# Building an adjacency matrix from one-hots: GpSimd takes over a third of the cell one-hots, and its additions move one group later

## The reference

```python
Z = jnp.matmul(X, W)
msg = Z[edge_src] * edge_vals[:, None]
agg = jax.ops.segment_sum(msg, edge_dst, num_segments=X.shape[0])
return jax.nn.relu(agg)
```

## Time and profile before

| | us |
|---|---|
| median of the runs shown (three) | 1432.24 |
| lowest and highest of them | 1429.69, 1436.95 |
| the profiled execution's own time | 1431.51 |
| its span, first to last instruction | 1429.8 |
| mean granted clock of TensorE | 0.979 |

### The profile page before, as it was taken

One profiled execution on the slowest core, in us unless ns is written; L12 is line 12 of the kernel. 1 busy time (PEld: TensorE's weight loads), 2 busy tenths in 40 slices (PEclk: granted clock), 3 DMA queues, 4 the chain that ended last, 5 costly groups with the idle time before them and its releaser, 6 DMA issues. The chain is left out here.

```text
span 1429.8 us, 23949 instructions
## 1 busy us (share of the span) xinstructions
PE 1365.1 (95%) x7919; PEld 892.0 (62%) x7920; DVE 771.4 (54%) x1622; ACT 457.2 (32%) x1133; POOL 261.9 (18%) x365
## 2 busy tenths in 40 slices
PE   9999999999999999999998999999989999889994
PEld 4688864455457777777555677767535555556661
DVE  7999965572158888877474333333360011643336
ACT  3599940021045555555112111111170012121110
POOL 1133320000000000000021555555200000005540
PEclk9999999999999999999999999999999999889996
DMA  6000000040000000000503999999510000543326
GB/s 159 30 0 0 0 0 0 0 180 0 0 30 2 2 1 2 1 2 1 162 15 95 328 317 316 320 322 306 173 54 0 0 0 0 174 164 96 102 82 227
DMA packets 84195, 131.01 MB, mean 92 GB/s; under 512 B 11865, under 2 KB 49135, under 8 KB 83733
## 3 DMA queue, kind: packets, MB, share of 16 engines
q1 hardware_dynamic: 70303, 108.72, 23.1%
q0 software_dynamic: 12032, 18.17, 4.0%
q10 hardware_dynamic: 1788, 3.16, 0.8%
HBM read 115.33 MB, written 29.56 MB: 101 GB/s over the span
## 5 line engine op out<-in xcount | busy, mean ns | idle before, releaser
L1267 PEld LDWEIGHTS ps<-b_r 128*128 128x128 f32 x1024 | 125.9, 194 | 34.5 <-issue 33.0
L1267 PE MATMUL ps<-b_r 128*128 128x78 f32 x1024 | 123.9, 275 | 2.0 <-DVE b_r L1344 1.3
L1276 PE MATMUL ps<-b_r 128*78 128x512 f32 x256 | 121.2, 596 | 0.0
L592 PE MATMUL ps<-b_r 125*125 125x160 f32 x660 | 118.4, 315 | 0.0
L1171 POOL TENSOR_TENSOR b_x<-b_x,b_r 125x512 f32<-125x512 f32 x10 | 12.7, 1267 | 534.5 <-DVE b_r L1121 534.5
L507 ACT ACTIVATE b_r<-b_r 125x125 f32<-125x125 f32 x330 | 107.6, 389 | 9.2 <-DVE b_r L402 4.8
L942 PEld LDWEIGHTS ps<-b_r 125*64 125x64 f32 x1600 | 85.3, 136 | 24.6 <-issue 22.8
L1327 ACT ACTIVATE b_r<-ps,b_r 128x78 f32<-128x78 f32 x128 | 34.7, 323 | 205.1 <-PE ps L1267 171.4
L905 PE MATMUL ps<-b_r 64*125 64x417 f32 (+1 forms) x480 | 95.4, 529 | 1.4 <-DVE ps L1034 1.2
L942 PE MATMUL ps<-b_r 125*64 125x125 f32 x1600 | 94.7, 272 | 1.3 <-ACT b_r L970 1.3
L592 PEld LDWEIGHTS ps<-b_r 125*125 125x125 f32 x660 | 92.0, 187 | 1.1
(11 more groups left out here) (272 smaller groups left out, 2224.3 us busy)
## 6 DMA issues: line engine op xcount, KB each, us to landing
b_r<-L_ffn_w SPq DMA_DIRECT2D x128, 512.0 KB
b_r<-y SPq DMA_DIRECT2D x20, 512.0 KB, 7.2
b_r<-L_ffn_W SPq DMA_DIRECT2D x2, 4096.0 KB, 20.4
y<-b_r SPq DMA_DIRECT2D x2, 2500.0 KB
rows<-b_r SPq DMA_DIRECT2D x2, 2400.0 KB
b_x<-x SPq DMA_DIRECT2D x5, 480.0 KB
out<-b_x ACTq DMA_DIRECT2D x5, 480.0 KB
b_w_a<-L_gnn_W SPq DMA_DIRECT2D x2, 512.0 KB, 9.3
```

Source lines behind the costliest of these rows:

```text
L592: last = pe.matmul(T.ps[:P, 2 + b, 0:WC], T.weighted[:, b, j, :], T.cells[:, b, j, :], start=(j == 0), stop=(j == CJ - 1))
L1267: last = pe.matmul(T.ps[:, 2 + r % 2, f * CAP:(f + 1) * CAP], T.ew1[r % WS][:, k, f * 128:(f + 1) * 128], T.ex_t[:, r % 2, k, :], start=(k ...
L1276: last = pe.matmul(T.ps[:CAP, 4 + r % 2, :], T.eh[:, r % 2, f, :], T.ew2[r % WS][:, f, :], start=(f == 0), stop=(f == FK - 1))
```

## The change

Three things change in this stage.

1. DVE's cells instruction makes two chunks (VJ = 2, 320 elements) instead of three. POOL makes the third chunk with a comparison of its own, `tensor_scalar` of 160 elements, against a column of one number for each edge. PE waits for it only ahead of the third of the count product's three matmuls, on a new semaphore `pool_cells`.
2. The numbers that POOL compares with are copied ten groups at a time into a small tile `ten_columns` (`next_columns`). That copy stands at the top of the loop's body. It waits until sources of the first of the ten groups has been made and until POOL's own previous comparison is done; everything on POOL waits for it (`columns_taken`).
3. POOL's weights addition for a group moves one group later against the rest: in the turn of group i POOL now adds group i-3, then makes the cells of group i. Both stand behind a wait for the weighted product of i-2. ACT's copy of the group one back now waits for one addition more, as counted. The window's start is loaded ahead of the waits, not behind the first of them. The last three additions stand behind the loop. In the first three groups, where there is nothing to add, POOL adds one column to itself instead. POOL's first ten groups are now written out separately, since the pass has an end of its own.

```diff
-    def column(columns, g, width):
-
-        return columns[:, bass.ds(g, 1), :].rearrange("e o j -> e (o j)").unsqueeze(2).to_broadcast([EC, CJ, width])
+    def column(columns, g, width, chunks=CJ):
+
+        return columns[:, bass.ds(g, 1), 0:chunks].rearrange("e o j -> e (o j)").unsqueeze(2)\
+            .to_broadcast([EC, chunks, width])
...
+            def next_columns(g0, seen):
+                pool.wait_ge(S.sources_ready, seen + 1)
+                pool.wait_ge(S.pool_cells, seen)
+                pool.tensor_copy(T.ten_columns, T.cell_col[:, bass.ds(g0, UNROLL), VJ]).then_inc(S.columns_taken, UNROLL)
+
+            def add_weights(g, b, seen, i):
+                load_start(pool, start, g)
+                sums = window(pool, T.at, start)
+                pool.wait_ge(S.weights_copied, seen + (i + 3))
+                pool.wait_ge(S.at_added, seen + (i + 3))
+                return sums, T.copied[:, b, :].rearrange("p (k d) -> p k d", k=NT)
+
             def body(g0, seen, first):
+                next_columns(g0, seen)
                 for i in range(UNROLL):
-                    pool.wait_ge(S.weights_copied, seen + (i + 3))
-                    load_start(pool, start, g0 + i)
-                    sums = window(pool, T.at, start)
-                    pool.wait_ge(S.at_added, seen + (i + 2))
-                    pool.tensor_tensor(sums, sums, T.copied[:, i % 2, :].rearrange("p (k d) -> p k d", k=NT), ALU.add)\
-                        .then_inc(S.at_added, 1)
-
-            pool.sem_inc(S.at_added, 2)
+                    adds = i >= 3 or not first
+                    if adds:
+                        sums, weights = add_weights(g0 + (i - 3), (i - 3) % 2, seen, i - 3)
+                    pool.wait_ge(S.columns_taken, seen + UNROLL)
+                    pool.wait_ge(S.products_done, seen + (i + 1))
+                    if adds:
+                        pool.tensor_tensor(sums, sums, weights, ALU.add).then_inc(S.at_added, 1)
+                    else:
+                        pool.tensor_tensor(T.taken[:, i:i + 1], T.ten_columns[:, i:i + 1], T.ten_columns[:, i:i + 1], ALU.add)
+                    pool.tensor_scalar(T.cells[:, i % 2, VJ], T.cell_iota, T.ten_columns[:, i:i + 1], None, ALU.is_equal)\
+                        .then_inc(S.pool_cells, 1)
+
+            def end_pass(seen):
+                for i in range(-3, 0):
+                    sums, weights = add_weights(NG + i, (NG + i) % 2, seen, i)
+                    pool.tensor_tensor(sums, sums, weights, ALU.add).then_inc(S.at_added, 1)
+
+            pool.sem_inc(S.at_added, 3)
...
-            visits(pool, "pool", body)
+            visits(pool, "pool", body, None, end_pass)
...
-                dve.wait_ge(S.at_added, r * NG + 2)
+                dve.wait_ge(S.at_added, r * NG + 3)
...
-                    dve.tensor_tensor(T.cells[:, b], cell_iota.unsqueeze(1).to_broadcast([EC, CJ, WC]),
-                                      column(T.cell_col, g, WC), ALU.is_equal).then_inc(S.cells_ready, 1)
+                    dve.tensor_tensor(T.cells[:, b, 0:VJ], cell_iota.unsqueeze(1).to_broadcast([EC, VJ, WC]),
+                                      column(T.cell_col, g, WC, VJ), ALU.is_equal).then_inc(S.cells_ready, 1)
...
-                act.wait_ge(S.at_added, seen + (i + 1))
+                act.wait_ge(S.at_added, seen + (i + 2))
...
                     for j in range(CJ):
+                        if j == VJ:
+                            pe.wait_ge(S.pool_cells, seen + (i + 1))
                         last = pe.matmul(T.ps[:P, b, 0:WC], T.sources_bf[:, b, j, :, 1], T.cells_bf[:, b, j, :, 1],
                                          start=(j == 0), stop=(j == CJ - 1))
...
-                pe.wait_ge(S.at_added, seen + 2)
+                pe.wait_ge(S.at_added, seen + 3)
```

More of the change, by code:

```diff
@@ L246, in graph_convolution @@
     BY_POOL, FIRST = 5000, 8000
+    VJ = CJ - 1
     PAIRS = NT // 2
@@ L1870, in semaphores_by_name @@
     S.counts_done, S.weighted_ready, S.sources_ready = semaphores("counts_done weighted_ready sources_ready")
+    S.pool_cells, S.columns_taken = semaphores("pool_cells columns_taken")
     S.products_done, S.cells_ready, S.weights_copied = semaphores("products_done cells_ready weights_copied")
@@ L2011, in program @@
             cut(EC, NG * CJ).rearrange("e (g j) -> e g j", j=CJ) for _ in range(7))
+        T.ten_columns, T.taken = cut(EC, UNROLL), cut(EC, 3)
         T.sources_bf = r6[:EC, 0:2 * CJ * P].bitcast(BF16).rearrange("e (b j s h) -> e b j s h", b=2, j=CJ, h=2)
```

## The result

The changed kernel takes 1447.6 us (median of 4 runs, 1446.6 to 1449.5), the kernel before 1433.2 (4 runs). The ratio is 1.0101, with a 95% interval of 1.0083 to 1.0119: slower by about 14 us. The forecast was slower too, but 1440, 8 us. Its own range of 1436 to 1444 missed; only the wide range of 1431 to 1450, whose upper part stood for rival C, holds the result. So the direction was right and the forecast size was little more than half of the measured one.

A forecast was written before the change was run, and what follows sets the result against it. The prediction took a ring through DVE's sequencer, ACT and PE, as tight as DVE itself, as the bound. Turns 7.65, last ten 0.9 and end -0.4 gave +8.2 us, so 1440; own range 1436 to 1444, wide range 1431 to 1450.

The forecast's parts named there:

- rival C: POOL becomes the bound in each group, from a comparison of 0.57 us on; 1446 at 0.7, 1453 at 0.84; chance 0.15.
- The stage is on the path whole: L610 starts when the last weights addition is done, so what a group costs counts 110 times.
- The ring, 3.72 for three groups: Loop through DVE's sequencer, ACT and PE closing after three groups: 3.76 us before, 3.72 after, 1.24 a group.
- Rival A: DVE was the bound, so a group would take 1.11 us; 1426 us, or 1418; chance 0.07.
- POOL's comparison, 0.42 us, bounds 0.18 and 0.51: POOL's new instruction, absent from the trace, priced between a one-element copy and the addition of 160.
- The prediction's second estimate, 0.45 or 0.32: POOL's comparison from the skill's cycles per element on top of the one-element copy; sum 1440.7 or 1439.4.
- Hidden with 0.16 to spare, decides from 0.57: POOL's chain in each group ends 0.16 us before PE needs the third chunk; a comparison of about 0.57 decides.
- The turn: Every ten groups POOL's chain waits for sources; weighted product 2.23 us after sources' end instead of 1.21; 0.85 a turn.
- PE's pace behind the turn: The group after a turn follows at PE's own pace, 1.11 us instead of 1.24.
- The end: End of the stage: the last addition starts about 0.2 us after the copy's end instead of 0.65; 0.4 won.
- The late addition costs nothing: ACT's copy waits for an addition ending well before the product of i-1 that it waits for anyway.
- The sum: Nine turn stretches 7.65, last ten 0.9, end -0.4: +8.2 us; ten groups 13.73 instead of 12.88.

The follow-up runs named there:

- e1: The kernel before, with DVE making two chunks of cells, the third left out (zeros) and POOL as before; ratio 0.9981.
- e5: The changed kernel, with POOL comparing 80 of the 160 numbers, the other half of the third chunk left out (zeros); 1441.5 us, ratio 1.0052.
- e13: The kernel before, with two chunks of cells on DVE, the third left out, and DVE's counts-window load moved behind the issue of sources; 1424.4 us, ratio 0.9928.
- e3: The changed kernel, with the copy of ten columns waiting for DVE's sources in the first ten groups alone; 1441.3 us, ratio 1.0051.
- e2: The changed kernel without POOL's comparison and copy of columns; DVE makes all three chunks, POOL's addition stays one group later; ratio 0.9996.
- e4: The changed kernel, with POOL comparing first in each group, the start's load and the weights addition behind it; ratio 1.0036.
- e10: The changed kernel, with the 160 numbers that POOL compares in fp32 instead of int16; one run, 1447.4 us.

## Why the prediction was right in direction and wrong in size

- *The stage is on the path whole.* Right: 12.3 of the 15.1 us between the two profiled executions are there at the start of L637.
- *The ring, 3.72 for three groups.* Right: 3.70 in e1, 3.72 in e5. Rival A fell with e1. Where the register load was taken out of the ring too (e13), groups came at 1.17, nearer to its 1.11, though not there.
- *POOL's comparison, 0.42 us, bounds 0.18 and 0.51.* This step failed: it measured 0.683, outside the bounds. I took the addition with two inputs for an upper end and weighed the select of 128 elements (0.28) most, but the comparison with a number per partition takes longer than the addition (0.50). The prediction's second estimate, 0.45 or 0.32, is off as well. The Trainium skill (GPSIMD Engine Reference, Engine selection) calls one-input work on GpSimd roughly line-rate. Here the measurement differs: about 2.5 ns for each further element (e5), where DVE's cells needs 1.1 (0.65 us for 480 elements, 0.48 for 320).
- *Hidden with 0.16 to spare, decides from 0.57.* The mechanism was right: rival C, with chance 0.15. By its formula a comparison of 0.683 gives 2.59 for two groups; measured 2.56. It adds 0.04 to 0.05 a group over the ring. C's own time of 1446 at a comparison of 0.7 left out that the longer comparison lengthens each turn as well.
- *The turn.* The weighted product starts 2.36 behind sources' end, forecast 2.23. The comparison adds 0.26, and the waits ahead of it cost 0.15 less than estimated (addition at 1.01 instead of 1.16). e5's ten groups of 13.61 support the term. e3 shows that only a third of the stall at 0.68 us is the wait for sources that I built it on; the chain behind it on POOL is the larger part.
- *PE's pace behind the turn* 1.13, forecast 1.11. *The end* 0.9 shorter, forecast 0.4: the load ahead gave 0.47, and 0.34 came on top because the last addition took 0.50 and not 0.84. Another 0.12 is a shorter way from it to L637 (0.25 instead of 0.37). The prediction put both long additions down to L364; the last one ran beside L373, which has both inputs in SBUF too, so the reading as contention stands. Which engine starts first was no term of the sum, so this gain was luck. *The late addition costs nothing*: right (e2), until its order is changed (e4).
- *The sum.* 13.73 for ten groups with 0.42 us, 14.12 measured. Of the missing 0.39, 0.13 is at the turn (2.36 for 2.23) and 0.26 in the groups between. Ten times 0.39 is 4 us: 8.2 + 4 = 12.2, the stage's share. The other 2 of the median's 14.4 lie within what the rest of the program varies.

## What to carry to other kernels

Before work moves off an engine that looks full, look for the ring that its saving would have to shorten: follow one result through all engines back to itself and divide by the groups between. A saving that isn't in that ring is worth next to nothing: here it was 0.11 us in ten groups, and 0.61 (0.84 less 0.23) once a register load was out of the ring. And where an operation has no row in the trace, its range should reach past the dearest neighbour, and the rival that starts there should have a chance to match.

## What the runs showed of the hardware

- GpSimd's comparison of a row with one number per partition: 0.68 us for 160 elements, in int16 (the changed kernel) as in fp32 (e10), and 0.48 for 80 in int16 (e5). Its addition of 160 with two inputs takes 0.50.
- A GpSimd addition and a DVE instruction with two inputs in SBUF that overlap cost the one that starts second: 0.84 us instead of 0.50 for GpSimd 0.01 behind L373 (before), 0.82 instead of 0.49 for DVE 0.04 behind GpSimd (the changed kernel).
- A register load from SBUF in an engine's instruction stream (medians of 0.29 us on GpSimd and 0.30 on VectorE) can sit in a ring between engines though the engine never looks idle. Before, it ran beside the engine's own instructions between turns, so no idle time named it there; it showed as idle time between turns only when those became shorter (e1).
- Engines' busy time falls when a chain between them binds (DVE 114 to 97 us in 117); before, three engines at 93 to 98% hid a ring that was as tight.
